# Another order of a head pair's steps: chosen rows' values and the second head's turn in their own pair, rows of maxima sent ahead of loads

## The chip, the cores and the metric

The kernel runs on one core of one Trainium2 chip. A core has five engines that each run a list of instructions of their own: TensorE (PE, matrix products and transposes; its weight loads are shown as PEld), VectorE (DVE), ScalarE (ACT), GpSimd (POOL) and SyncE (SP), which here only sends transfers to 16 DMA engines. They wait for one another by semaphores. The metric is the device time of one execution in microseconds (us), lower is better.

## What is computed

A transformer layer on 2 x 1024 tokens of 512 numbers: LayerNorm, attention with 16 heads of 32, LayerNorm and residual, then a mixture of 8 experts with a shared part, LayerNorm and residual. The edit touches the attention only:

```python
ctx = _local_attention(q, k, v)      # each block of 128 queries sees 256 keys around it
idx = _global_index(q)               # 62 rows with the largest norm of q, the first and the last row
qg = jnp.take_along_axis(q, idx[..., None], axis=-2)
g_scores = jnp.einsum('nhqd,nhkd->nhqk', qg, k) / math.sqrt(d)     # 64 chosen rows see all 1024 keys
g_probs = jax.nn.softmax(g_scores, axis=-1)
g_ctx = jnp.einsum('nhqk,nhkd->nhqd', g_probs, v)
ctx = ctx.at[bn, bh, idx].set(g_ctx)
x = x + _layernorm(ctx_as_tokens, axis=-1)
```

## The kernel before

Three stages follow one another. The projections of q, k and v (to about 169 us) write them to HBM, split in high and low parts. The attention (169 to 384 us) takes the 2 x 16 heads in 16 pairs. The experts take the rest. While the attention runs, the slots of each pair hold chores of the other stages: the search for the largest norms of the second batch (pairs 0 to 5, on VectorE), loads of expert weights, and from pair 10 on the LayerNorm of finished tokens.

A head has these steps. Its queries and keys are loaded by SyncE, three DMAs each (load_queries, load_keys); values come for two pairs at a time (load_values). TensorE makes the scores once for the maximum of each row (row_max, two units into a 1024 wide buffer), VectorE takes the maxima (row_reduce), TensorE turns them (row_shift), ScalarE copies them out (row_copy) and SyncE sends them as row 96 of the query tile (row_send). With this row in place TensorE makes the transposed, shifted scores (local_scores, four units), ScalarE the exponentials (local_exp), TensorE the products with the values (local_values), ScalarE copies them (local_out), TensorE turns them back (local_turn), VectorE divides (local_finish). After every fourth head SyncE stores the results (store_heads).

The chosen rows are done for the two heads of a pair together: gather and stack_split on GpSimd, stack_q on TensorE, stack_copy on ScalarE, global_scores, global_max, global_exp, three global_turn with three global_turned, global_values, global_out, global_back, global_finish, and scatter_rows into the stored result.

Which step stands where is written by hand, for each engine one list per pair: pair_on_pe, pair_on_act, pair_on_dve, pair_on_pool and pair_on_sp. The calls head(name, n, s, ...) and pair(name, n, ...) put the step of head 2n + s, or of pair n, at that place; slot(k) holds the chores. An engine works through its list in order, so a step that must wait holds up all that stands behind it, and a DMA is sent only when SyncE comes to it. Buffers are rings: ST_ (three banks, taken by local_scores, row_shift, stack_q, global_turn, global_back and LayerNorm turns, in TensorE's order), W_ (two wide buffers, taken by row_max, global_scores, global_values), O_ (one bank: local_values and local_turn), six query and six key tiles (QSe, KSe, QSl, KSl, and four that lie in the tiles WQH and WKH). Whoever takes a buffer waits until its last user is done. Most matrix products have one line, L1216, so they are told apart by their tiles: bank<-QS,KS are local_scores, wide<-KS,QS row_max, bank<-PT,VS local_values, wide<-KS,GT global_scores, wide<-PTG,VS global_values, bank<-twice global_back. L1311 is row_shift, L1317 stack_q, L1350 local_turn, L1374 global_turn, L1225 the turn of a LayerNorm tile.

Of the kernel before, what the change touches and what calls it, by code (L numbers as in the profile page):

```python
# [117 lines left out]
def sandwich(nc, x, wq, bq, wk, bk, wv, bv, wg, w1, w3, w2, s1, s3, s2, out):  # L118
# [16 lines left out]
    with ExitStack() as top:  # L135
# [253 lines left out]
        def places():  # L389
# [361 lines left out]
            def last_tile():  # L751
                hold["st", 15] = STC.take()
                for c in range(2):
                    hold["last", c] = UP.take()

            walk(locals())


# [7 lines left out]
        def walk(steps, engine=None):  # L766

            def do(name, *a):
                if name in steps:
                    steps[name](*a)  # L770
# [94 lines left out]
            def head(name, n, s, *a):  # L865
                h = 2 * n + s
                if (4 if name[:4] == "load" else 2 if name[:3] == "row" else 0) <= h < 32:
                    do(name, h, *a)

            def pair(name, n, *a):  # L870
                if name == "load_values":
                    if n % 2 == 0 and 2 <= n < 16:
                        do(name, n // 2)
                elif name == "scatter_rows":
                    if n % 2 == 1 and 0 <= n < 16:
                        do(name, n // 2)
                elif {"gather": 8, "stack_split": 2}.get(name, 0) <= n < 16:
                    do(name, n, *a)

            def pair_on_pe(i, slot):  # L880
                pair("global_values", i - 1)
                slot(0)
                slot(1)
                head("local_scores", i, 0, 1)
                head("local_turn", i - 1, 1)
                pair("global_scores", i)
                pair("global_back", i - 1)
                head("local_scores", i, 0, 2)
                head("row_max", i + 1, 0, 1)
                slot(2)  # L890
                head("local_scores", i, 0, 3)
                head("local_scores", i, 1, 0)
                slot(3)
                head("local_values", i, 0, 0)
                head("local_values", i, 0, 1)
                head("local_values", i, 0, 2)
                head("local_values", i, 0, 3)
                head("row_shift", i + 1, 0)
                head("row_max", i + 1, 1, 0)
                pair("global_turn", i, 0)  # L900
                slot(4)
                head("local_scores", i, 1, 1)
                head("local_turn", i, 0)
                head("local_scores", i, 1, 2)
                head("row_max", i + 1, 1, 1)
                head("local_scores", i, 1, 3)
                pair("global_turn", i, 1)
                slot(5)
                pair("stack_q", i + 1)
                head("local_values", i, 1, 0)  # L910
                head("local_values", i, 1, 1)
                head("local_values", i, 1, 2)
                head("local_values", i, 1, 3)
                head("row_max", i + 2, 0, 0)
                head("local_scores", i + 1, 0, 0)
                pair("global_turn", i, 2)
                head("row_shift", i + 1, 1)
                slot(6)
                slot(7)

            def pair_on_act(i, slot):
                slot(0)
                pair("global_out", i - 1)
                slot(1)
                head("local_exp", i, 0, 1)
                head("local_exp", i, 0, 2)
                slot(2)
                slot(3)
                head("local_exp", i, 0, 3)
                pair("global_exp", i)  # L930
                head("local_exp", i, 1, 0)
                head("row_copy", i + 1, 0)
                head("local_out", i, 0)
                pair("global_turned", i, 0)
                head("local_exp", i, 1, 1)
                slot(4)
                head("local_exp", i, 1, 2)
                slot(5)
                head("local_exp", i, 1, 3)
                pair("global_turned", i, 1)  # L940
                pair("stack_copy", i + 1)
                head("local_exp", i + 1, 0, 0)
                head("row_copy", i + 1, 1)
                pair("global_turned", i, 2)
                slot(6)
                head("local_out", i, 1)
                slot(7)

            def pair_on_dve(i, slot):
                slot(0)  # L950
# [14 lines left out]
                head("row_reduce", i + 2, 0, 0)  # L965

            def pair_on_pool(i, slot):
                pair("gather", i + 2)
                slot(0)
                slot(1)  # L970
                pair("stack_split", i + 1)
                pair("scatter_rows", i - 2)
                slot(2)
                slot(3)
                slot(4)
                slot(5)
                slot(6)
                slot(7)

            def pair_on_sp(i, slot):  # L980
                slot(0)
                slot(1)
                slot(2)
                head("store_heads", i - 1, 1)
                head("load_keys", i + 3, 0)
                head("row_send", i + 1, 0)
                pair("load_values", i + 2)
                slot(3)
                slot(4)
                slot(5)  # L990
                slot(6)
                head("load_queries", i + 2, 1)
                head("load_keys", i + 2, 1)
                head("row_send", i + 1, 1)
                head("store_heads", i, 0)
                head("load_queries", i + 3, 0)
                slot(7)

            pair_on = {"PE": pair_on_pe, "ACT": pair_on_act, "DVE": pair_on_dve, "POOL": pair_on_pool, "SP": pair_on_sp}

            def pairs(engine, with_chores=True):
# [210 lines left out]
        def tensor_program(pe):  # L1212
# [277 lines left out]
            def attention_over():  # L1490
                PE["ended"] = PE["end"]

            walk(locals(), "PE")

        def scalar_program(sc):
# [181 lines left out]
            def attention_over():  # L1679
                ACTE["ended"] = ACTE["end"]  # L1680

            walk(locals(), "ACT")


# [794 lines left out]
```

## Time and profile before

| | us |
|---|---|
| time, median of 3 | 806.63 |
| lowest, highest | 806.3, 814.18 |
| profiled execution | 810.11 |
| its span | 808.4 |
| TensorE busy | 773.3 |
| VectorE busy | 562.5 |
| ScalarE busy | 420.8 |
| GpSimd busy | 145.4 |

Busy times are sums over an engine's instructions; matmuls overlap their weight loads and their ends are modelled, so a share near 100% doesn't mean that TensorE is at its peak. A timeline row gives the start, the length from the start of the first to the end of the last of its instructions, the engine, the line, the operation with its tiles, and in brackets the idle time before it and what ended it. The granted clock of TensorE is 1.00 in all of the attention stage up to 380 us.

### The profile page before, as it was taken

To read this page: it belongs to the slowest core of one execution; us is meant where nothing else is said; L and a number is where in the kernel's file an instruction comes from. 1 tells how busy PE (TensorE), PEld (TensorE's weight loads), DVE (VectorE), ACT (ScalarE), POOL (GpSimd) and SP (SyncE) were. 2 spreads that over 40 slices of the span, in tenths; PEclk is the share of its full clock that TensorE was granted. 3 is DMA by queue.
4 is the path that set the end of the run, shared out by engine and by line. 5 is a ranking of instruction groups with operands and counts; after the bars stand their busy time and mean duration, and the time that the engine had idled before them with its cause. 6 is when DMAs were issued, how large, how long until landed. Compare 5 with 4: busy or idle time off the path is not lost. (4 is left out here: it accounts for less than half of the span.)

```text
span 808.4 us, 13818 instructions
## 1 busy us (share of the span) xinstructions
PE 773.3 (96%) x5077; PEld 650.2 (80%) x5077; DVE 562.5 (70%) x1200; ACT 420.8 (52%) x840; POOL 145.4 (18%) x229
## 2 busy tenths in 40 slices
PE   6999999999999999999999998999999999999994
PEld 4787787777777777787878886999999999887884
DVE  5764898578897567777588445566676666758676
ACT  5464352445656566677354343666676666633120
POOL 3300010510101213233254422000000000013122
PEclk9999999999999999999999999999999999999998
DMA  7789565976766798862259432586778786546444
GB/s 233 227 273 349 187 181 177 271 221 175 217 183 183 179 255 244 236 179 82 94 194 337 185 132 70 179 261 211 211 206 265 207 263 208 170 152 200 139 157 144
DMA packets 117636, 162.39 MB, mean 201 GB/s; under 512 B 17380, under 2 KB 65508, under 8 KB 117568
## 3 DMA queue, kind: packets, MB, share of 16 engines
q1 hardware_dynamic: 113984, 153.54, 62.7%
q0 software_dynamic: 3584, 7.97, 3.3%
q8 instruction: 40, 0.66, 0.3%
q14 instruction: 28, 0.23, 0.1%
HBM read 107.24 MB, written 55.05 MB: 201 GB/s over the span
## 5 line engine op out<-in xcount | busy, mean ns | idle before, releaser
L1576 ACT ACTIVATE PT<-bank 128x512 f32<-128x512 f32 x128 | 74.2, 596 | 54.7 <-PE bank L1216 50.5
L1216 PE MATMUL wide<-W2H,HH 128*128 128x512 f32 x308 | 100.7, 392 | 0.5 <-ACT OUTR L1501 0.5
L1984 DVE TENSOR_TENSOR SIL<-bank,SIL 128x256 f32<-128x256 f32 (+1 forms) x72 | 36.8, 512 | 70.9 <-ACT SIL L1661 70.5
L1661 ACT ACTIVATE SIL<-bank 128x256 f32<-128x256 f32 (+1 forms) x72 | 32.6, 453 | 100.4 <-PE bank L1216 95.3
L1216 PE MATMUL bank<-XT,W13H 128*128 128x256 f32 (+1 forms) x336 | 76.6, 322 | 0.0
L1501 ACT ACTIVATE HH<-SIL 128x256 fp32r<-128x256 f32 (+1 forms) x72 | 35.2, 489 | 64.8 <-DVE SIL L1984 64.8
L1216 PEld LDWEIGHTS wide<-W2H,HH 128*128 128x128 f32 x308 | 57.8, 188 | 13.0 <-ACT OUTR L1501 1.3
L1216 PE MATMUL wide<-W2L,HH 128*128 128x512 f32 x168 | 65.8, 391 | 0.4 <-DVE W2L L1895 0.4
L1986 DVE TENSOR_TENSOR HH<-SIL,HH 128x256 fp32r<-128x256 f32 (+1 forms) x72 | 37.0, 514 | 39.9 <-ACT HH L1501 38.5
L1216 PEld LDWEIGHTS bank<-XT,W13H 128*128 128x128 f32 x336 | 55.0, 188 | 4.7
L1216 PE MATMUL bank<-WQL,W13H 128*128 128x256 f32 (+1 forms) x168 | 55.5, 330 | 0.0
L1216 PE MATMUL bank<-WKL,W13H 128*128 128x256 f32 (+1 forms) x168 | 54.3, 323 | 0.0
L1216 PE MATMUL bank<-WQL,W13L 128*128 128x256 f32 (+1 forms) x168 | 54.1, 322 | 0.0
L1216 PE MATMUL bank<-XT,W13L 128*128 128x256 f32 (+1 forms) x168 | 53.6, 319 | 0.0
L2098 POOL TENSOR_TENSOR STC<-STC,mhalf 128x1 f32<-128x1 f32 x47 | 28.4, 604 | 134.4 <-DVE STC L1695 133.8
L2202 POOL DMA_INDIRECT H2A<-scr_oe,FG x8 | 8.0, 996 | 209.7 <-issue 209.7
L1891 DVE TENSOR_TENSOR W13L<-R,W13H 128x512 fp32r<-128x512 f32 x70 | 44.1, 685 | 1.7 <-ACT W13H L1501 1.7
L1216 PE MATMUL bank<-XT,WQH 128*128 128x256 f32 (+1 forms) x192 | 43.0, 319 | 0.0
L1216 PE MATMUL bank<-WVH,HT 128*128 128x512 f32 x128 | 41.7, 415 | 0.7 <-DVE HT L1717 0.6
L1895 DVE TENSOR_TENSOR W2L<-R,W2H 128x512 fp32r<-128x512 f32 x60 | 41.1, 686 | 1.5
L1216 PE MATMUL bank<-HT,WKH 128*128 128x512 f32 x128 | 41.0, 402 | 0.0
L1216 PE MATMUL bank<-HT,WQH 128*128 128x512 f32 x128 | 40.8, 400 | 0.0
(303 smaller groups left out, 2066.2 us busy)
## 6 DMA issues: line engine op xcount, KB each, us to landing
R<-in_L_ffn_W_dram SPq DMA_DIRECT2D x48, 512.0 KB, 5.3
scr_q<-hl SPq DMA_DIRECT2D x16, 512.0 KB, 3.7
scr_k<-hl SPq DMA_DIRECT2D x16, 512.0 KB, 4.0
R<-in_L_ffn_sw_dram SPq DMA_DIRECT2D x12, 512.0 KB, 5.0
QSe<-scr_q SPq DMA_DIRECT2D x36, 128.0 KB
KSe<-scr_k SPq DMA_DIRECT2D x36, 128.0 KB
R<-_attn_hidden_states_dram SPq DMA_DIRECT2D x16, 256.0 KB, 3.7
scr_qtok<-H2A SPq DMA_DIRECT2D x16, 256.0 KB, 3.7
```

Of the source, the lines that this page charges most:

```text
L1216: return pe.matmul(ps, a, b, start=start, stop=stop, skip_group_check=True)
L1501: return sc.activation(dst, src, ACT.Copy)
L1576: sc.activation(pt.buf[:, :], hold["s", n, u].buf[:, :], ACT.Exp, scale=SCALE).then_inc(*a_exp.up(n, u))
L1661: sc.activation(sil.buf[r, 0:N], a_in, ACT.Silu).then_inc(*a_inner.up("silu", q, m))
L1891: dv.tensor_tensor(lo, rb[:, :, c * P:(c + 1) * P], f(hi), ALU.subtract).then_inc(*d_split.up("13", j, c))
L1895: dv.tensor_tensor(W2L[:, m, :], r2[:, m, :], f(W2H[:, m, :]), ALU.subtract).then_inc(*d_split.up("2", j, m))
L1984: dv.tensor_tensor(sil[r, 0:N], b_in, sil[r, 0:N], ALU.mult).then_inc(*d_inner.up("mul", q, m))
L1986: dv.tensor_tensor(lo, sil[r, 0:N], f(HH[r, 0, m, 0:N]), ALU.subtract).then_inc(*d_inner.up("lo", q, m))
L2098: po.tensor_tensor(st[:, 2:3], st[:, 3:4], mhalf[:, :], ALU.pow).then_inc(*g_pow.up(*key))
L2202: po.indirect_dma_start(out=ga.buf, out_offset=None, in_=oed, in_offset=bass.IndirectOffsetOnAxis(ap=FG[:, t:t + 1], axis=0)).then_inc(*l_ ...
```

## The change

The lists of four engines get another order; VectorE's list is as before. No step is added or removed.

```diff
             def pair_on_pe(i, slot):
-                pair("global_values", i - 1)
+                head("local_scores", i, 0, 1)
+                pair("global_back", i - 1)
                 slot(0)
+                pair("global_scores", i)
                 slot(1)
-                head("local_scores", i, 0, 1)
-                head("local_turn", i - 1, 1)
-                pair("global_scores", i)
-                pair("global_back", i - 1)
                 head("local_scores", i, 0, 2)
                 head("row_max", i + 1, 0, 1)
...
                 pair("global_turn", i, 0)
-                slot(4)
                 head("local_scores", i, 1, 1)
                 head("local_turn", i, 0)
                 head("local_scores", i, 1, 2)
+                slot(4)
                 head("row_max", i + 1, 1, 1)
+                pair("global_turn", i, 1)
                 head("local_scores", i, 1, 3)
-                pair("global_turn", i, 1)
+                head("row_max", i + 2, 0, 0)
+                pair("stack_q", i + 1)
                 slot(5)
-                pair("stack_q", i + 1)
                 head("local_values", i, 1, 0)
                 head("local_values", i, 1, 1)
                 head("local_values", i, 1, 2)
                 head("local_values", i, 1, 3)
-                head("row_max", i + 2, 0, 0)
+                head("row_shift", i + 1, 1)
+                pair("global_turn", i, 2)
+                slot(6)
                 head("local_scores", i + 1, 0, 0)
-                pair("global_turn", i, 2)
-                head("row_shift", i + 1, 1)
-                slot(6)
+                pair("global_values", i)
                 slot(7)
+                head("local_turn", i, 1)
 
             def pair_on_act(i, slot):
...
                 head("local_exp", i, 1, 0)
+                head("local_out", i, 0)
                 head("row_copy", i + 1, 0)
-                head("local_out", i, 0)
                 pair("global_turned", i, 0)
                 head("local_exp", i, 1, 1)
+                head("local_exp", i, 1, 2)
                 slot(4)
-                head("local_exp", i, 1, 2)
                 slot(5)
                 head("local_exp", i, 1, 3)
                 pair("global_turned", i, 1)
                 pair("stack_copy", i + 1)
+                head("local_out", i, 1)
+                head("row_copy", i + 1, 1)
+                slot(6)
+                pair("global_turned", i, 2)
+                slot(7)
                 head("local_exp", i + 1, 0, 0)
-                head("row_copy", i + 1, 1)
-                pair("global_turned", i, 2)
-                slot(6)
-                head("local_out", i, 1)
-                slot(7)
...
             def pair_on_pool(i, slot):
-                pair("gather", i + 2)
                 slot(0)
                 slot(1)
+                pair("scatter_rows", i - 2)
+                pair("gather", i + 1)
+                slot(2)
+                slot(3)
                 pair("stack_split", i + 1)
-                pair("scatter_rows", i - 2)
...
             def pair_on_sp(i, slot):
                 slot(0)
                 slot(1)
+                head("load_keys", i + 2, 1)
                 slot(2)
-                head("store_heads", i - 1, 1)
-                head("load_keys", i + 3, 0)
+                pair("load_values", i + 2)
                 head("row_send", i + 1, 0)
-                pair("load_values", i + 2)
                 slot(3)
                 slot(4)
                 slot(5)
                 slot(6)
-                head("load_queries", i + 2, 1)
-                head("load_keys", i + 2, 1)
+                head("load_keys", i + 3, 0)
+                head("store_heads", i, 0)
                 head("row_send", i + 1, 1)
-                head("store_heads", i, 0)
+                head("load_queries", i + 2, 1)
+                head("store_heads", i, 1)
                 head("load_queries", i + 3, 0)
                 slot(7)
```

On TensorE, the end of pair 1 and the start of pair 2, from stack_q on, stood before as:

```order
L1317 MATMUL bank<-ident,GS 96x128
L1216 MATMUL bank<-PT,VSe 33x256 x6
L1216 MATMUL bank<-PT,VSe 33x128 x4
L1216 MATMUL wide<-KSl,QSe 128x192
L1216 MATMUL wide<-KSl,QSe 128x256 x3
L1216 MATMUL bank<-QSl,KSl 128x256 x2
L1374 MATMUL bank<-ident,PG 128x128
L1311 MATMUL bank<-ident,MX 72x128
L1216 MATMUL wide<-PTG,VSe 64x128 x9
L1216 MATMUL bank<-QSl,KSl 128x256 x2
L1350 MATMUL bank<-ident,OS 128x97 x4
L1216 MATMUL wide<-KSl,GT 128x512
```

and stand now as:

```order
L1216 MATMUL wide<-KSe,QSe 128x192
L1216 MATMUL wide<-KSe,QSe 128x256 x3
L1317 MATMUL bank<-ident,GS 96x128
L1216 MATMUL bank<-PT,VSe 33x256 x6
L1216 MATMUL bank<-PT,VSe 33x128 x4
L1311 MATMUL bank<-ident,MX 72x128
L1374 MATMUL bank<-ident,PG 128x128
L1216 MATMUL bank<-QSl,KSl 128x256 x2
L1216 MATMUL wide<-PTG,VSe 64x128 x9
L1350 MATMUL bank<-ident,OS 128x97 x4
L1216 MATMUL bank<-QSl,KSl 128x256 x2
L1216 MATMUL bank<-twice,OS 128x64
```

The row_max of the next pair but one went ahead of the products with the values, row_shift stands right behind them, and the turn-back of the chosen rows ahead of the next pair's scores of chosen rows.

On SyncE, after the first loads into late buffers (pair 0), a row of maxima is DMA ...<-MR. Before:

```order
L2283 DMA QSl0<-scr_q 32x1024 x3
L2292 DMA KSl1<-scr_k 32x1024 x3
L2309 DMA WQH<-MR2 1x8x128
L2301 DMA VSl<-scr_v 64x136
L2302 DMA VSl<-scr_v 128x7x136
L2304 DMA VSl<-scr_v 64x136
L2283 DMA QSl1<-scr_q 32x1024 x3
L2292 DMA KSe0<-scr_k 32x1024 x3
L2309 DMA WQH<-MR3 1x8x128
```

and now:

```order
L2283 DMA QSl0<-scr_q 32x1024 x3
L2292 DMA KSl1<-scr_k 32x1024 x3
L2301 DMA VSl<-scr_v 64x136
L2302 DMA VSl<-scr_v 128x7x136
L2304 DMA VSl<-scr_v 64x136
L2309 DMA WQH<-MR2 1x8x128
L2292 DMA KSe0<-scr_k 32x1024 x3
L2309 DMA WQH<-MR3 1x8x128
L2283 DMA QSl1<-scr_q 32x1024 x3
L2283 DMA QSe0<-scr_q 32x1024 x3
```

The row of head 2 went behind the values, the row of head 3 ahead of three loads of queries.

Around the first store of four heads (scr_ctx<-CT0), from a row of maxima on, SyncE sent before:

```order
L2309 DMA QSl1<-MR1 1x8x128
L2283 DMA WQH<-scr_q 32x1024 x3
L2351 DMA R13<-in_L0_ffn_sw1_dram 128x4x256
L2319 DMA scr_ctx<-CT0 128x8x128
L2292 DMA WKH<-scr_k 32x1024 x3
```

and now:

```order
L2309 DMA QSl1<-MR1 1x8x128
L2283 DMA QSe1<-scr_q 32x1024 x3
L2319 DMA scr_ctx<-CT0 128x8x128
L2283 DMA WQH<-scr_q 32x1024 x3
L2351 DMA R13<-in_L0_ffn_sw1_dram 128x4x256
L2292 DMA WKH<-scr_k 32x1024 x3
```

The queries of the tile WQH, which stood right behind the row, now stand behind three other loads and the store.

## Rows read from the trace of the kernel before

**Rows 1.** The page, part 1: busy us, share of the span, number of instructions.
```profile
PE 773.3 (96%) x5077; PEld 650.2 (80%) x5077; DVE 562.5 (70%) x1200; ACT 420.8 (52%) x840; POOL 145.4 (18%) x229
```

**Rows 2.** Windows: length; busy PE, PEld, DVE, ACT, POOL; clock; DMA share; GB/s.
```profile
206.20:247.06 40.86, 40.08 (x356) 31.26 (x355) 37.18 (x72) 25.72 (x58) 4.68 (x8) 1.00 0.74 201
287.98:313.88 25.90, 25.78 (x239) 20.48 (x237) 16.61 (x39) 17.03 (x39) 4.00 (x6) 1.00 0.88 244
```

**Rows 3.** Timeline of TensorE in pairs 2 and 3.
```profile
206.20 0.27 PE L1317 MATMUL bank<-ident,GS 128*96 128x128 f32 x1
...
211.61 0.50 PE L1216 MATMUL wide<-KSl,GT 96*128 96x512 f32 x1
...
216.50 0.30 PE L1311 MATMUL bank<-ident,MX 128*72 128x128 f32 x1
216.70 0.70 PE L1216 MATMUL wide<-KSl,WQH 96*128 96x192 f32 x4
```

**Rows 4.** Timeline of VectorE in the same pair.
```profile
211.48 1.20 DVE L1768 MAX8 TV<-NRM 16x8 f32<-16x1024 f32 x1
...
213.91 1.22 DVE L1842 TENSOR_REDUCE SG<-wide 128x1 f32<-128x1024 f32 x1
...
216.10 0.35 DVE L1822 TENSOR_REDUCE MX<-wide 128x1 f32<-128x192 f32 x1
217.44 0.36 DVE L1817 TENSOR_REDUCE MX<-wide 128x1 f32<-128x192 f32 x1 [1.00 <-PE wide L1216]
```

**Rows 5.** Timeline of TensorE from stack_q in pair 10 to stack_q in pair 14.
```profile
313.88 0.27 PE L1317 MATMUL bank<-ident,GS 128*96 128x128 f32 x1
...
320.83 0.60 PE L1225 MATMUL bank<-ident,H2A 128*128 128x128 f32 x4
321.18 0.58 PE L1216 MATMUL bank<-QSl,WKH 97*128 97x128 f32 x3
322.15 0.50 PE L1216 MATMUL bank<-QSl,KSe 97*128 97x256 f32 x2 [0.38 <-DMA QSl<-MR]
...
365.18 0.27 PE L1311 MATMUL bank<-ident,MX 128*72 128x128 f32 x1 [0.34 <-DVE WKL L1885]
...
368.37 0.27 PE L1317 MATMUL bank<-ident,GS 128*96 128x128 f32 x1
```

**Rows 6.** Timeline of SyncE's sending in pair 10.
```profile
315.18 0.37 SPq L2335 DMA_DIRECT2D scr_x<-XX  x1
...
317.01 1.40 SPq L2292 DMA_DIRECT2D WKH<-scr_k  x3
318.45 0.68 SPq L2309 DMA_DIRECT2D QSl<-MR  x1
```

**Rows 7.** Timeline of SyncE's sending in pair 0.
```profile
175.05 1.35 SPq L2283 DMA_DIRECT2D QSl<-scr_q  x3
...
177.83 0.65 SPq L2309 DMA_DIRECT2D WQH<-MR  x1
178.53 0.51 SPq L2301 DMA_DIRECT2D VSl<-scr_v  x1
...
179.70 0.58 SPq L2304 DMA_DIRECT2D VSl<-scr_v  x1
...
183.26 0.68 SPq L2309 DMA_DIRECT2D WQH<-MR  x1
```

**Rows 8.** Timeline of TensorE: first scores of head 2, and of head 3.
```profile
180.75 0.51 PE L1216 MATMUL bank<-WQH,WKH 97*128 97x256 f32 x2 [0.78 <-DMA WQH<-MR]
...
187.14 0.50 PE L1216 MATMUL bank<-WQH,WKH 97*128 97x256 f32 x2 [1.44 <-DMA WQH<-MR]
```

**Rows 9.** Keys behind the store; DMA issues, 180 to 385: KB each, us to landing.
```profile
200.19 2.46 SPq L2292 DMA_DIRECT2D WKH<-scr_k  x3
...
WKH<-scr_k SPq DMA_DIRECT2D x24, 128.0 KB, 4.8
...
VSl<-scr_v SPq DMA_DIRECT2D x3, 476.0 KB
```

More of the change, by code:

```diff
@@ L967, in pair_on_pool @@
             def pair_on_pool(i, slot):
-                pair("gather", i + 2)
                 slot(0)
                 slot(1)
-                pair("stack_split", i + 1)
                 pair("scatter_rows", i - 2)
+                pair("gather", i + 1)
                 slot(2)
                 slot(3)
+                pair("stack_split", i + 1)
                 slot(4)
@@ L991, in pair_on_sp @@
                 slot(6)
+                head("load_keys", i + 3, 0)
+                head("store_heads", i, 0)
+                head("row_send", i + 1, 1)
                 head("load_queries", i + 2, 1)
-                head("load_keys", i + 2, 1)
-                head("row_send", i + 1, 1)
-                head("store_heads", i, 0)
+                head("store_heads", i, 1)
                 head("load_queries", i + 3, 0)
```

## The prediction

> **What bounds the kernel now.** I read the page's busy times first: TensorE is busy for 96% of the span [rows 1]. That does not yet say that it sets the pace everywhere, since a matmul's end is modelled; the edit touches only the attention stage (about 169 to 384 us), so I cut that stage into windows and looked at which engine waits for which.
>
> The first windows differ in kind [rows 2]. From 206.20 to 247.06, three head pairs take 40.86 us, 13.62 each, and VectorE is busy for 37.18 of it (91%): this is where it also looks for the largest norms of the second batch. From 287.98 to 313.88 two pairs take 25.90, 12.95 each, TensorE is busy for 25.78 and VectorE for 16.61. So there are two regimes: VectorE sets the pace up to about 247 us, TensorE after that.
>
> What closes the circle in the first regime is seen by laying TensorE's timeline beside VectorE's. VectorE's row_reduce(i+1,0,1) ends at 216.45; row_shift follows on TensorE at 216.50, row_max(i+1,1,0) behind it at 216.70; VectorE sits idle for 1.00 us and takes that product at 217.44 [rows 3, 4]. Everything else in VectorE's pair stands back to back. A pair is thus VectorE's work plus this 1.00, and TensorE has 13.62 - 12.95 = 0.67 us of slack in it, which it spends in small waits, such as that for the reduction of the buffer (VectorE goes on at 211.48, chosen scores start at 211.61).
>
> After 313.88 the clean pair of 12.95 gets four transposes of a LayerNorm tile, 0.35 us (320.83 to 321.18), so 13.30. The four pairs from 313.88 to 368.37 take 54.49, 13.62 each [rows 5]: 0.32 too much in each, 1.3 in all. Two of them wait for a row of maxima (0.38 at 322.15, the next one is alike), two for VectorE (0.34 at 365.18).
>
> **The change, part by part.**
>
> *Values of the chosen rows and the second head's turn, in their own pair; chosen rows' turn-back ahead of the scores (TensorE, ScalarE).* No matmul is added or removed. In the VectorE regime nothing moves: VectorE's own list is the same in both kernels, and the three instructions on which it waits each pair (row_reduce, row_shift, row_max in a row) keep their neighbours. global_back a microsecond earlier frees VectorE's global_finish, but VectorE reaches it late anyway: it starts its reduction of the chosen scores at 213.91, long after the scores began at 211.61. Term: 0.0. It would only be other than 0 if a wait of more than 0.67 us per pair came in on TensorE.
>
> In the TensorE regime global_back ahead of the scores lets VectorE begin about half a microsecond sooner on the maximum, the row_reduce behind it and the LayerNorm step at the end; the 0.34 waits for VectorE go, and they are no longer than that half microsecond. Bounds: 0 and all the excess of these pairs.
>
> *Rows of maxima ahead of loads (SyncE).* In pair 10 SyncE waits for the LayerNorm store until 315.18, then sends three loads of queries and three of keys, and only at 318.45 the row; TensorE needs it and gets it at 322.15, 3.7 us later [rows 6]. In the new order only three loads stand between that store and the row, so it goes 1.4 us sooner, more than the wait of 0.38. Both DMA waits go. With the part above: -1.3 us, the whole excess, the other end being 0. I take the whole, since each wait is shorter than what is gained on its own releaser.
>
> *The other side of that: what is now ahead of a row.* row_send(i+1,0) is sent behind the values in every second pair. In the steady stage it doesn't matter: the row is sent a third into the pair and used at its end. At the start it does. All loads into late buffers wait for one fence and then come in a burst; the row of head 2 is sent at 177.83 and its first scores start at 180.75, after a wait; the row of head 3 is sent at 183.26 and used at 187.14 after a wait of 1.44 [rows 7, 8]. In the new order the three loads of values (178.53 to 180.28, 1.8 us of sending) come ahead of the row of head 2: it is sent at about 179.6. Rows took 2.9 and 3.9 us from sending to use; behind the values (476 KB and two of 34, 544 in all [rows 9]) I take the longer: 183.5. Then TensorE has to do what lies between local_scores(1,0,0) and local_scores(1,1,0): 180.75 to 185.7 (187.14 less the wait of 1.44) is 4.95, less 0.3 for two transposes that now stand before it: 188.1 against 187.14. The row of head 3 is sent earlier than now (row_shift right behind the values' products) and has landed by then. Term: +1.0 us; bounds 0.0 (row lands after 2.9) and +2.0 (a microsecond later still). Also row_max(2,0,0) now stands before the second head's values and waits for queries that are sent from 175.05 on; that wait ends near 179 and lies inside the one for the row.
>
> The Trainium skill speaks against this edit: "DMA: Bandwidth & Descriptors", section "Queues, rings and completion order", says that on each DMA engine descriptors are consumed in ring order, so a small row can't pass the 544 KB ahead of it. By the rule the term is the +1.0 or more; without it the row would land after its 2.9 us and the term would be 0. The trace agrees as far as it goes: behind six loads a row of 4 KB took 3.9 us.
>
> *Queries later.* Queries of head (i+3,0) are now sent behind the store of four heads (512 KB) in odd pairs, and row_max(i+2,0,0), which needs them, stands 1.86 us of products sooner. In the old order keys stand behind that store: sent from 200.19 to 202.65, and loads of that form take 4.8 us to land [rows 9], so near 206.7. TensorE would be at that row_max at 206.20, the place of stack_q now. A wait of 0.5 us in three pairs of the VectorE regime is inside the slack of 0.67: 0.0. In the TensorE regime the store is sent earlier in the pair, since VectorE, whose division comes before it, isn't behind: 0.0. Upper bound: 1.0 us in each of six pairs.
>
> *GpSimd.* The gather moves from a pair ahead to just before its split and behind the scatter. The row of indices is there two microseconds or more before stack_q; 0.0, at most 0.3 in two odd pairs.
>
> **Sum.** 0.0 + 1.0 - 1.3 + 0.0 = -0.3 us on the attention stage. Later stages start from its end and move with it. The profiled execution took 810.11 us outside, 808.4 of span, 3.5 above the median of 806.63; the difference goes onto the median: 806.3.
>
> **Rivals.**
>
> A. *As forecast*, small terms of both signs: 805 to 808. Chance 0.62.
>
> B. *The queries are late.* TensorE waits at row_max(i+2,0,0) in pairs 2, 4, 6 and 8, 10, 12. With 1.0 us each: 3 x (1.0 - 0.67) + 3 x 1.0 = +4.0, 810.3: slower than before. It decides from 0.67 us of wait in the first three, from the first tenth in the others. For it: DMA engines are busy for 0.74 to 0.88 of these windows [rows 2]. Against: the hand count gives 0.5 and 0. Chance 0.17, of which 0.07 for waits near 2 us, 3 x 1.33 + 3 x 2 = +10, 816.
>
> C. *The VectorE regime is shortened too.* If VectorE's wait of 1.00 went, six pairs would come down by 0.67: -4.0, with the -1.3 and no loss at the start 801.3. Against: the neighbours row_shift and row_max are unchanged. Chance 0.13, with 0.03 for yet more.
>
> D. *ScalarE is late.* The copy of the chosen rows' product (global_out) must lie between global_values and global_back, and only the turn and one unit of scores are left there, 0.6 us, where the scores of the chosen rows stood too. If this costs 0.15 in ten pairs: +1.5, 807.8. Chance 0.08.
>
> **How the numbers follow.** About 1% (8 us) is what a measurement of this kernel can tell from no change. All the waits named here together are 4.0 of slack in six pairs, 1.3 late and 0.78 + 1.44 at the start, 7.5 us, so faster by over 1% gets 0.03, a part of C. Slower by over 1% needs the heavy end of B: 0.07. The rest, 0.90, is within 1%. The range of 801 to 811.5 takes in A, D, C and B's middle; outside it are the heavy end of B and the tail of C.
>
> **What would show it.** Right: pairs of 13.6 us up to 247, VectorE's 1.00 before L1817 still there; no wait for MR rows after 313 and pairs of 13.3 there; a longer wait for WQH<-MR near 183. Wrong: TensorE idle before row_max on the wide buffers until a load of QS (B); VectorE's idle time before L1817 gone (C); L1216 bank<-twice waiting for ScalarE's OS (D).

## The result, and the profile after

| | ratio to before, 95% interval | median us (lowest to highest) | profiled execution, its span | TensorE busy |
|---|---|---|---|---|
| before | 1 | 808.08 (806.3 to 814.18) | 810.11, 808.4 | 773.3 |
| changed | 1.0311 [1.0238, 1.0385] | 834.74 (830.31 to 837.67) | 834.02, 832.3 | 783.3 |

The changed kernel is 3.1% slower, some 26 us, where 806.3 with a range up to 811.5 had been forecast. The page of after, part 1 and the clock of part 2 (busy us and share of the span as in [rows 1]; below it the granted clock in 40 slices of 20.8 us, in tenths, 9 for 90% and more):

```profile
PE 783.3 (94%) x5077; PEld 658.7 (79%) x5077; DVE 562.6 (68%) x1200; ACT 421.9 (51%) x840; POOL 145.7 (18%) x229
...
PEclk9999999999799987999999999999999999999998
```

Against [rows 1] VectorE, ScalarE and GpSimd did the same work to within a microsecond, but TensorE was busy for 10 us longer with the same 5077 products. So the loss has two parts, waiting and slower work. Behind the attention nothing was lost: its last part was 424 us before and is 421 now. All that is sought lies in the attention stage, which ends 27 us later.

TensorE's waits in that stage (engine, line, what was waited for; us in all, times, longest):

```profile
PE bank L1216 <- DMA QSe<-MR: 8.4, 2, 5.0
PE bank L1216 <- DMA QSl<-MR: 6.6, 2, 4.0
PE bank L1216 <- DMA WQH<-MR: 3.8, 2, 2.9
PE wide L1216 <- DMA QSl<-scr_q: 1.8, 1, 1.8
```

Six waits for a row of maxima, 18.8 us, and one of 1.8 for queries at the start; all the others are small. They stand at one step, local_scores(i+1, 0, 0), and only in the stretches in which SyncE also sends values. Windows of after from stack_q to the next stack_q; the second is the first such stretch with a wait (columns as in [rows 2]):

```profile
193.68:207.32 13.64, 13.17 (x120) 10.37 (x119) 12.42 (x24) 8.57 (x20) 2.16 (x3) 1.00 0.56 153
207.32:228.21 20.89, 17.47 (x120) 13.43 (x119) 12.44 (x25) 8.71 (x20) 0.81 (x4) 0.75 0.70 162
228.21:241.83 13.62, 13.17 (x121) 10.37 (x119) 12.40 (x25) 8.57 (x20) 2.23 (x4) 1.00 0.54 152
241.83:257.22 15.39, 12.79 (x120) 10.18 (x119) 12.52 (x24) 8.63 (x20) 0.72 (x3) 1.00 0.89 210
...
300.75:324.20 23.45, 18.48 (x121) 14.22 (x119) 7.69 (x17) 8.47 (x20) 1.08 (x3) 0.71 0.61 155
```

The stretches between them are as forecast (13.64, 13.62) or better. The ones with values, in us:

| stretch from stack_q of pair | 2 | 4 | 6 | 8 | 10 | 12 | sum |
|---|---|---|---|---|---|---|---|
| before | 13.58 | 13.65 | 14.46 | 13.02 | 13.70 | 13.53 | 81.94 |
| after | 20.89 | 15.39 | 17.20 | 23.45 | 18.81 | 14.38 | 110.12 |
| wait for the row in it | 3.42 | 2.60 | 2.87 | 4.97 | 4.04 | 0.91 | 18.81 |
| granted clock in it | 0.75 | 1.00 | 0.90 | 0.71 | 0.91 | 1.00 | |

They are 28.2 us longer in all; the other stretches together give 1.9 back and the start takes 0.7, which makes the 27. In pairs 4 and 12, where the clock stays at 1.00, a stretch grows by no more than its wait. In pairs 2 and 8, where it falls for long, it grows by twice as much. (The 14.46 of before in pair 6 hold a wait of 1.03 us for VectorE that the same list of TensorE doesn't show in experiment 10, 13.02, so that this pair's loss is put too low by about that.) TensorE's timeline of after around that of pair 2:

```profile
209.38 0.30 PE L1311 MATMUL bank<-ident,MX 128*72 128x128 f32 x1
209.52 0.27 PE L1374 MATMUL bank<-ident,PG 128*128 128x128 f32 x1
213.21 0.50 PE L1216 MATMUL bank<-QSe,KSe 97*128 97x256 f32 x2 [3.42 <-DMA QSe<-MR]
...
219.48 1.32 PE L1216 MATMUL bank<-QSe,KSe 97*128 97x128 f32 x5
220.73 3.63 PE L1216 MATMUL bank<-PT,VSl 128*33 128x256 f32 x20
...
225.58 0.48 PE L1216 MATMUL bank<-QSe,KSe 97*128 97x256 f32 x2
```

The products with the values take 3.63 us here and 1.93 at the full clock: the lower of the two clock levels (granted clock 0.50 in windows of 2 us from 216 to 224, 0.69 and 0.75 in those beside them), for some 10 us behind a wait of 3.42. In pairs 6 and 10 the means of 0.90 and 0.91 come to some 3.4 us at the lower level.

And SyncE's sending of after before that wait:

```profile
200.36 0.38 SPq L2319 DMA_DIRECT2D scr_ctx<-CT  x1
200.79 2.20 SPq L2283 DMA_DIRECT2D WQH<-scr_q  x3
203.03 0.43 SPq L2351 DMA_DIRECT2D R<-in_L_ffn_sw_dram  x1
203.56 1.37 SPq L2292 DMA_DIRECT2D WKH<-scr_k  x3
205.03 0.51 SPq L2301 DMA_DIRECT2D VSe<-scr_v  x1
205.58 0.58 SPq L2302 DMA_DIRECT2D VSe<-scr_v  x1
206.21 0.62 SPq L2304 DMA_DIRECT2D VSe<-scr_v  x1
206.87 0.68 SPq L2309 DMA_DIRECT2D QSe<-MR  x1
```

The row goes at 206.87 and is there at 213.2, 6.3 us later. The same place in the kernel before, and the first scores that need the row:

```profile
197.06 1.37 SPq L2283 DMA_DIRECT2D WQH<-scr_q  x3
198.47 0.43 SPq L2351 DMA_DIRECT2D R<-in_L_ffn_sw_dram  x1
199.71 0.38 SPq L2319 DMA_DIRECT2D scr_ctx<-CT  x1
...
203.64 0.64 SPq L2309 DMA_DIRECT2D QSe<-MR  x1
...
208.83 0.40 PE L1216 MATMUL bank<-QSe,KSl 97*128 97x256 f32 x2
```

Queries and weights went ahead of the store, three loads of keys behind it (200.19 [rows 9]), and then nothing: SyncE waited for the row itself, sent it at 203.64, and sent the values behind it. What that pause did is seen in the busy share of the DMA engines (tenths). Before from 203 to 209 us, then after from 206 to 213 us, 40 slices each; in both the row is sent in the fifth slice:

```profile
DMA  9999999795644110005304558999999999998599
```

```profile
DMA  9999999999597979979999999999999999899989
```

Before, the engines ran dry 1.3 us behind the row's sending. After, they stay full until well past its landing.

### The profile page after: what moved, and what is told of

It reads as the page before. It is cut to its first block and busy times, and to the rows that moved or that the text cites. A ratio compares the mean times of both kernels' runs of the same rounds, so it can differ in the third digit from the quotient of the medians.

```text
span 832.3 us, 13846 instructions
## 1 busy us (share of the span) xinstructions
PE 783.3 (94%) x5077; PEld 658.7 (79%) x5077; DVE 562.6 (68%) x1200; ACT 421.9 (51%) x840; POOL 145.7 (18%) x229
```

## The experiments

In the comparison above and the three below, the kernel before took 808 to 815 us (chips differ), so the ratios count, not the microseconds.

**1. The row ahead of the values, nothing else.**

```diff
-                pair("load_values", i + 2)
                 head("row_send", i + 1, 0)
+                pair("load_values", i + 2)
```

> The changed kernel with one swap on SyncE: row_send(i+1, 0) goes ahead of load_values(i+2) instead of behind it. Theory Q (a queue): the lost time comes from that row alone, which in every second pair is sent 1.85 us later and then lies behind 544 KB of values. Then in pair 2 it goes at about 205.0 and lands some 3 us later, before TensorE needs it at 209.8; the waits of 3.42, 2.60, 2.87, 4.97, 4.04 and 0.91 us for a row of maxima in the pairs 2 to 12 go, the granted clock stays at 1.00, and the time is 804 to 808. Rival S (the store and what stands behind it): the row is late because SyncE waits for the store of four heads at 200.36 and then sends seven loads ahead of it; only the 1.85 us of sending come off, waits of 1 to 3 us remain and the time is 815 to 825. Rival T (the order on TensorE): the time stays above 830.

Measured 810.06, ratio 0.9984 [0.9955, 1.0013]: one swap takes away all of the loss. Four waits of this row remain: 0.84 us in pair 2 (the stretch takes 13.62 all the same), 1.22, 1.59 and 0.52 later; behind the one of 1.59, in pair 10, the granted clock fell to 0.90 for the stretch, which takes 16.39. Theory Q holds for the size; S is right only in that a small rest stays.

**2. The reverse: the kernel before, with the values ahead of the row.**

> The kernel before with one swap on SyncE: load_values(i+2) ahead of row_send(i+1, 0). This is the step of which the prediction said that it doesn't matter in the steady stage. As the prediction has it: 806 to 808. Theory Q: the row of pair 2, ready at 203.6, goes at about 205.5 instead of 203.64 and needs 5 us and more behind the values, so it is there at about 211; the kernel before wants it at 208.83. That is 2 us of wait in each of six pairs, less 0.67 of slack in three of them: +8 to +12, 815 to 820, and above that if the granted clock falls behind the waits. Rival S: the values alone do little, below 811.

Measured 820.45, ratio 1.0087 [1.0057, 1.0117]. The direction is theory Q's and the step of the prediction is wrong, but theory Q said too much for the early pairs: in pair 2 the wait is 0.59 us and the stretch 13.76, in pair 4 there is no wait for it. Of the profiled execution's loss 5.6 us lie at the start (a wait of 3.34 for the row of head 2, and the clock falls behind it) and 2.8, 3.3 and 1.2 in pairs 6, 8 and 10. So the values alone don't make 3%. They do it on top of something that the changed list adds and this one doesn't.

**3 and 4. The SyncE lists exchanged.**

> The changed kernel with the whole SyncE list of before, the lists of TensorE, ScalarE and GpSimd as changed. Theory Q or S (SyncE's list holds the whole loss): 803 to 808, the late pairs a little shorter than before (12.7 to 13.3 us). Rival T (TensorE's new order holds a part of it): above 812.

Measured 808.39, ratio 0.9953 [0.9909, 0.9997], span 804.5 against 808.4.

> The kernel before with only the SyncE list changed. Theory Q or S: 820 to 840, waits for a row of maxima in every second pair. Rival T: below 815.

Measured 844.17, ratio 1.0417 [1.0378, 1.0457], with seven waits for rows, 20.3 us. Rival T falls: the whole loss is in SyncE's list, and the new order of TensorE, ScalarE and GpSimd is by itself a small gain, if any (the interval ends at 0.9997). With the old order of TensorE the new SyncE list is even worse: its stretches with values are as long as in the changed kernel (109.8 us), but the row of head 2 is waited for at the start (3.73 us; the start takes 3.1 more) and the stretches without values take 1.8 more.

**6 and 7. Bytes or sending time?** The three loads of values are split around the row.

```diff
                 pair("load_values", i + 2)
                 head("row_send", i + 1, 0)
+                pair("values_rest", i + 2)
```

> The changed kernel, but of the three loads of values only the two small ones (34 KB each) are sent ahead of row_send(i+1, 0); the one of 476 KB goes behind it. If it is the 544 KB ahead of the row that count: near the kernel with the row ahead of all values, 808 to 813. If it is the time that SyncE needs to send three loads (1.85 us, of which two thirds remain): 818 to 826.

> The changed kernel, but of the three loads of values only the one of 476 KB is sent ahead of row_send(i+1, 0), the two small ones behind it. If it is the bytes that count: near the changed kernel, 826 to 835. If it is the time that SyncE needs for sending (a third of it remains): 812 to 818.

With 68 KB ahead of the row: ratio 0.9997 [0.9964, 1.003]. With 476 KB ahead: 1.0266 [1.0216, 1.0316]. Two sends of 34 KB keep SyncE busy for longer than one of 476 KB (1.1 us against 0.4), and the time shows no cost of them. It is the bytes. (The profiled execution with 68 KB does have waits: five for this row, of 0.4 to 2.2 us, and in pair 9 one of 2.44 us for queries before row_max, which is the prediction's rival B; it did not occur in the changed kernel.)

**9. The values in another queue.**

```diff
             def pair_on_act(i, slot):
...
                 head("local_exp", i, 0, 3)
+                pair("values_act", i + 2)
                 pair("global_exp", i)
```

> The changed kernel, but from pair 2 on ScalarE sends the three loads of values, behind local_exp(i, 0, 3), about 1.5 us before SyncE comes to row_send(i+1, 0). The row still has the 544 KB of values started ahead of it on the same 16 DMA engines, but in another queue. If what holds the row is the order within SyncE's queue: it lands some 3 us after it is sent, as in the kernel before, and the time is 804 to 814, ScalarE's sending included. If it is the DMA engines themselves, which the values keep busy whoever sends them: waits of 2 us and more for rows of maxima stay in the even pairs, 820 to 835.

Measured 821.77, ratio 1.0143 [1.0099, 1.0187], between the two theories in size, and much of it lies elsewhere. ScalarE's global_exp now comes some 2 us late, and TensorE waits 0.8 to 1.0 us for it in six stretches without values. In the profiled execution the stretches without values lose 5.2 us, those with values 5.7, and the start 7.7 (a wait of 2.62 for the row of head 2, and the clock at 0.68 behind it), though SyncE sends the values there as in the changed kernel. The landing tells more. SyncE and TensorE in pair 2 of this kernel:

```profile
212.93 0.64 SPq L2336 DMA_DIRECT2D QSe<-MR  x1
...
219.72 0.50 PE L1222 MATMUL bank<-QSe,KSe 97*128 97x256 f32 x2 [0.84 <-DMA QSe<-MR]
```

The row takes 6.8 us with no values ahead of it in its own queue, and 6.6 in pair 8. In pair 2 SyncE's own queue holds ahead of it what it holds in experiment 1. From the store's sending to the first scores it is 10.3 us there (199.11 to 209.38), 12.3 here (207.46 to 219.72) and 12.9 in the changed kernel. So the values in ScalarE's queue delay the row by 2 us, nearly what they cost in its own; order within SyncE's queue is not enough to explain that.

**A sum for all of them.** After these runs I counted what is ahead of the row from the store on (SyncE waits for VectorE before it): store 512 KB, keys 384; in the changed list also queries 384, expert weights 512 and values 544. At the 243 GB/s that a window of before shows,

```profile
202.00:210.00 8.00, 7.85 (x81) 6.26 (x79) 6.93 (x13) 5.65 (x14) 2.52 (x4) 1.00 0.86 243
```

and 2.9 us for the row itself [rows 7, 8], the first scores can start at (1 KB is 1024 bytes):

| kernel, pair 2 | store sent | KB ahead | sum gives | first scores |
|---|---|---|---|---|
| 1, row ahead | 199.11 | 1792 | 209.6 | 209.38 |
| 6, 68 KB ahead | 199.16 | 1860 | 209.9 | 209.44 |
| 7, 476 KB ahead | 200.80 | 2268 | 213.3 | 212.31 |
| changed | 200.36 | 2336 | 213.1 | 213.21 |
| 4, new SyncE list | 203.58 | 2336 | 216.3 | 215.47 |
| 9, values on ScalarE | 207.46 | 2336 | 220.2 | 219.72 |
| 2, before with values ahead | 205.48 | 1440 | 214.5 | 215.37 |

All seven are within a microsecond; the sum was made after the runs, so this is a fit and no forecast. Number 9 comes out only if the values of the other queue are counted: without them the sum gives 217.9 in pair 2 and 247.2, 275.7 and 303.2 in pairs 4, 6 and 8, with them 249.5, 278.0 and 305.5, and the scores started at 248.97, 277.31 and 305.24.

The start of the count matters in the lists of before. There the queries and weights (896 KB) are sent just ahead of the store, 197.06 to 198.9, and are not done when the store goes. Counted from 197.06, 1792 KB end at 204.6, which is where the slices above fall, so the row, sent at 203.64, can be there at 207.5, 1.3 us before 208.83 where it is needed. Experiment 2 counted so gives 215.6 in pair 2 (215.37 measured) and 270.3 in pair 6 (270.05), where the count from the store would give 268.4. Two places stay off: in pair 8 of the changed kernel the sum gives 305.9 and the row came at 308.2, and in pair 8 of experiment 2 it is 301.1 against 302.6, so there something is left over that isn't found.

This also explains why 2 cost so little and 1 gained so much. The 1.3 us to spare in before take more than half of the 2.3 us that the values need (544 KB at that rate). In the changed list the queries and weights had already used them up: sent behind the store, they leave the DMA engines less to do before it (share 0.39 in 197 to 199 us of before) and more between it and the row, and even without the values the row comes late by 0.84 us (experiment 1).

**5. Is the clock a cost of its own?** 26 transposes of a constant in each of five waits.

```diff
+                if r == 2 and i in (2, 4, 6, 8, 10):
+                    for k in range(26):
+                        c = (1 + k % 3) * P
+                        pe.transpose(tb.buf[:, c:c + P], ident[:, :], ident[:, :])
                 for k, t in enumerate(TILES[r]):
```

> The changed kernel, with 26 transposes of a constant that nobody reads ahead of global_turn(i, 2) in the pairs 2, 4, 6, 8 and 10, where TensorE waits for the row of maxima anyway; at the 0.35 us of four such transposes they are 2.3 us of work in each. Theory K (the clock adds to the waits): the waits of the changed kernel are 18.8 us in all, but the even pairs are 29.1 us longer than before; the rest is TensorE at half speed behind the wait (values in 3.63 instead of 1.93 us). With TensorE busy in the wait the granted clock stays at 1.00 in more of these pairs, pair 2 comes from 20.89 down to about 17, pair 8 from 23.45 to about 18.5, and the whole takes 822 to 828 although work was added. Rival (the waits alone, the work behind them is slow for another reason, such as late copies or a busy memory): 833 to 840.

Measured 828.4, ratio 1.0158 [1.0111, 1.0204]: useless work was added, and half of the loss went. Its profiled execution took 835.87 us, more than its median, so I read stretches and not its end. TensorE in pair 2, and two windows, pairs 2 and 8:

```profile
209.94 3.00 PE L1375 MATMUL bank<-ident 128*128 128x128 f32 x26
212.78 0.27 PE L1378 MATMUL bank<-ident,PG 128*128 128x128 f32 x1
213.34 0.50 PE L1216 MATMUL bank<-QSe,KSe 97*128 97x256 f32 x2 [0.29 <-DMA QSe<-MR]
...
218.19 1.93 PE L1216 MATMUL bank<-PT,VSl 128*33 128x256 f32 x20
```

```profile
207.74:223.65 15.91, 15.62 (x147) 13.03 (x145) 12.45 (x25) 9.02 (x20) 0.84 (x4) 1.00 0.81 202
...
296.44:312.59 16.15, 15.61 (x146) 12.92 (x146) 8.00 (x18) 8.75 (x19) 1.35 (x3) 1.00 0.89 224
```

The row is as late as in the changed kernel (213.34, and 213.21 there). But TensorE was busy meanwhile, the clock stayed at 1.00, and the stretch takes 15.91 instead of 20.89. So of the 7.3 us that this stretch had lost, 5.0 were the clock and 2.3 the wait. Theory K holds for pairs 2 and 8. (Its expectation has the stretches 29.1 us longer than before; by the table it is 28.2.) The cure is no better than the wait in every place. In pair 4, where the clock had not fallen, the row came later still behind the filler (a wait of 1.55) and the stretch takes 17.19 for 15.39; in pair 10 of the same execution a wait of 2.94 us stood behind the filler, and the clock fell to 0.78 for that stretch, 23.54 us; pair 12, without filler, takes 17.99. The six stretches with values together are only 3 us shorter here than in the changed kernel (107.0 for 110.1), so what the clock costs is shown for two pairs and not for the whole. The Trainium skill, "TensorE: Matmul & The Clock Gate", section "HAM oscillation — how this bites in real kernels", describes such a loop: waits for a DMA between bursts of products bring the throttled clock back each time. The trace agrees for four waits of the changed kernel (0.71 to 0.91 in their stretches) and not for those of 2.60 and 0.91 us, behind which it stayed at 1.00. The length of the wait doesn't decide it: the clock also fell behind 2.07 us (experiment 7, pair 2, 0.74 in the stretch) and 1.59 (experiment 1, pair 10), and stayed at 1.00 behind 3.10 (experiment 2, pair 8).

**8 and 12. A version that beats both.** The lists of experiment 3, and on VectorE, where it waits for row_max:

```diff
                 slot(4)
+                if i < 6:
+                    slot(5)
                 head("row_reduce", i + 1, 1, 0)
                 head("local_finish", i, 0)
-                slot(5)
+                if i >= 6:
+                    slot(5)
```

> Meant to beat both: TensorE, ScalarE and GpSimd as changed, SyncE as before (which took 808.39 against 812.88 in the same runs), and on VectorE in the pairs 0 to 5 one step of the search for the largest norms (1.2 us) stands ahead of row_reduce(i+1, 1, 0), in the 1.00 us in which VectorE waits there. By the reading of the prediction (a pair of these is VectorE's work and that wait, TensorE has 0.67 us of slack) the pairs 2 to 6 come from 13.6 down to 12.95 or so: 3 to 4 us less than e3_old_sync. Rival: the step pushes row_reduce(i+1, 1, 0) and what hangs on it (row_max two units on, the row of the second head) back by as much as it gains: no change against e3_old_sync.

> e8_chore_in_gap again, the same kernel, beside the two above and with more rounds: 0.983 to 0.990 of the kernel before. If the first result was partly the chip's doing, it comes nearer to the ratio of the two profiled spans, 800.0 to 808.4, 0.990.

Measured 802.37, ratio 0.985 [0.9805, 0.9895], and the second time 801.1, 0.9899 [0.9858, 0.994]. One stretch of the early pairs, where before had 13.6:

```profile
193.06:205.55 12.49, 12.49 (x120) 10.13 (x119) 12.27 (x24) 8.56 (x20) 0.00 (x0) 1.00 0.71 194
```

TensorE is busy for all of it, and VectorE for 12.27. The others of the early pairs take 12.48 to 12.86.

**10. The same on the kernel before.**

> The kernel before, with VectorE's step of the search for the largest norms ahead of row_reduce(i+1, 1, 0) in the pairs 0 to 5, nothing else. It prices the 1.00 us that VectorE waits in each of these pairs, with TensorE's old order: by the prediction's reading TensorE has 0.67 us of slack, so the pairs come from 13.6 to 12.95 and not below, -3 to -4 us in all, and the 12.49 of e8_chore_in_gap are due to TensorE's new order. If instead the pairs here come down to 12.5 too, TensorE's order has nothing to do with it.

Measured 805.12, ratio 0.9947 [0.9922, 0.9972]. Three early pairs, to be laid beside the first row of [rows 2]:

```profile
205.42:244.12 38.70, 38.52 (x356) 30.86 (x355) 36.85 (x72) 25.71 (x58) 4.99 (x8) 1.00 0.79 211
```

12.90 a pair, as the reading of the two regimes had it (12.95), and not 12.49. The rest of experiment 8 is the new order of TensorE, ScalarE and GpSimd; the next experiment shows a part of it at work, in the pairs that VectorE doesn't bound.

**11. The turn-back of the chosen rows ahead of the scores, alone.**

```diff
-                pair("global_scores", i)
                 pair("global_back", i - 1)
+                pair("global_scores", i)
```

> The kernel before with one swap on TensorE: global_back(i-1) ahead of global_scores(i). This is the part that the prediction credited with the end of the 0.34 us waits for VectorE in the late pairs. If it is right: no wait of row_shift for VectorE after 313, pairs 12 and 14 shorter by 0.3 us, 0.7 in all, no change in the pairs up to 247. If it is wrong: those waits stay, and the shorter pairs of e3_old_sync (12.5 to 13.1 where there were 12.9 to 13.5) come from other parts of TensorE's list.

The two waits of row_shift for VectorE, 0.7 us before, are gone behind 313, but the two stretches with them are shorter by 0.14 and 0.11 only, where 0.3 each had been expected. What was not expected: the stretches of pairs 7 to 9, which had no marked wait, take 12.6 us where they took 12.9 to 13.0. VectorE in one of these, before:

```profile
307.47 0.51 DVE L1854 TENSOR_SCALAR GC<-bank,SG 64x32 f32<-64x32 f32 x2 [0.45 <-PE bank L1216]
...
310.21 0.35 DVE L1822 TENSOR_REDUCE MX<-wide 128x1 f32<-128x192 f32 x1
```

and TensorE behind it, again before:

```profile
308.64 1.93 PE L1216 MATMUL bank<-PT,VSl 128*33 128x256 f32 x20
310.61 0.30 PE L1311 MATMUL bank<-ident,MX 128*72 128x128 f32 x1
310.81 0.70 PE L1216 MATMUL wide<-KSe,QSl 96*128 96x192 f32 x4
```

The same with the swap:

```profile
304.55 0.51 DVE L1854 TENSOR_SCALAR GC<-bank,SG 64x32 f32<-64x32 f32 x2
...
307.28 0.35 DVE L1822 TENSOR_REDUCE MX<-wide 128x1 f32<-128x192 f32 x1
```

```profile
306.12 1.93 PE L1216 MATMUL bank<-PT,VSl 128*33 128x256 f32 x20
307.97 0.30 PE L1311 MATMUL bank<-ident,MX 128*72 128x128 f32 x1
308.03 0.72 PE L1216 MATMUL wide<-KSe,QSl 96*128 96x192 f32 x4
```

Before, VectorE waits 0.45 us for global_back, ends its reduction at 310.56, and row_shift comes 1.97 us behind the start of the values' products and row_max 0.20 behind that; now VectorE is done at 307.63, and it is 1.85 and 0.06. That is 0.26 us of TensorE's time in this pair, in waits too short for the trace to mark. Timed the swap is 810.14, ratio 0.9996 [0.9966, 1.0025], so what the traces show (0.3 us in each of three pairs, 0.1 to 0.35 in three of the later ones, and 0.56 lost in pair 10) is below what the timing can tell.

## Why the prediction was wrong, step by step

**The step that failed** is one sentence: "In the steady stage it doesn't matter: the row is sent a third into the pair and used at its end." Already for the old order the reading is wrong: from the row's sending to its use it was 5.2 us (203.64 to 208.83) in a pair of 13.65, so the row went some 60% of the way in and not a third. The step also takes the moment of sending from the old order, in which SyncE pauses for the row, and it takes a landing of about 3 us for granted. In the new order the row goes 3.2 us later (206.87 against 203.64) and needs 6.3 us, where TensorE came for it 2.9 us behind its sending. The term stood at nothing; the stage paid 27 us, nearly all of it here: 18.8 of waits, and lower clock behind four of them (5.0 us in pair 2, by experiment 5).

**The rule was at hand and used in one place.** The prediction weighed the Trainium skill's "DMA: Bandwidth & Descriptors", section "Queues, rings and completion order", by which each DMA engine takes the descriptors of a ring in order, for the start, where it gave +1.0. The same 544 KB stand ahead of the same kind of row in six more pairs. Experiments 6 and 7 agree with the rule. Experiment 9 goes beyond it: 6.8 us with the values in the other queue.

**What else was ahead of the row** wasn't counted. "Queries later" was costed only for who needs the queries; nobody did have to wait for them in the steady stage, as forecast. That 384 KB of queries and 512 KB of weights had moved from ahead of the store to behind it, between SyncE's wait at the store and the row, was not in the sum. The share of 0.74 and 0.88 of busy DMA engines was cited for rival B only, and spoke for this case much more.

**The start** was right in size by luck and wrong in place. Forecast +1.0; from the first stack_q to the third, at the end of pair 1, it was 0.7 us longer (24.99 against 24.30). The row of head 2 went at 179.63, forecast 179.6, and the scores started at 182.89, forecast 183.5, with no wait at the row. The wait was at row_max, for its queries (1.75 us, until 178.98), which the prediction had put inside the other one. Behind it the granted clock fell to 0.50 (181.5 to 183.5 us), and the products with the values took 2.82 us, which the prediction didn't have either.

**Two regimes and the slack** were right. 13.64, 13.62 and 13.54 us in the three early stretches without values; a wait of 2.60 in pair 4 cost 1.7, its length less 0.9, near the 0.67 of slack; and experiment 10 came to 12.90 for 12.95.

**The -1.3** for the late pairs was right in sign where no values are sent. In the changed kernel the stretches without values from pair 7 on take 12.79, 12.69, 13.02 and 12.65 for 12.91, 12.88, 13.76 and 13.50 before. The other half of the term, that no wait for a row is left behind 313, failed: pairs 10 and 12 wait 4.04 and 0.91 us for it. The part on global_back named the right mechanism (VectorE's wait of 0.45 us goes in experiment 11), but applied it only to the 0.34 us waits. The "clean pair" of 12.95 was not clean: 0.3 us of unmarked waits went with the swap.

**Rivals.** In the changed kernel B (queries), C and D did not occur. D did in other runs with TensorE's new order: waits of 0.3 to 1.1 us of global_back for ScalarE in experiments 1, 3, 6 and 8, such as 0.73 and 0.34 in experiment 3. That slower by over 1% got 0.07, all of it from B, is the consequence of the failed step: the mechanism that decided was not among the rivals.

What stays open: the 2.3 us by which the row of pair 8 came later than the sum, the exact share of the clock in the pairs other than 2, and what decides behind which waits it falls.

## What to carry to other kernels

In this kernel a small, urgent transfer had to be priced by the bytes sent since the DMA engines were last idle, over the rate that the windows show, whoever sent them; not by its place in the list. It is worth doing this sum first. A pause of the sending engine just ahead of it can be what makes it fast, and loads that fill such a pause must go behind it. Where a wait of some microseconds falls on a TensorE that is otherwise busy, look at the granted clock behind it before setting the loss to the length of the wait; and before moving a step, ask of every wait on another engine what could stand in it.

## What the runs showed of the hardware

The clock behind a wait cost more than the wait itself in pair 2: 5.0 us behind one of 3.42, taken back by 26 transposes that nobody reads. The length of a wait doesn't tell whether the clock falls: 3.10 us (experiment 2) and 2.60 left it at 1.00, while 2.87, 2.07 (experiment 7) and 1.59 (experiment 1) were followed by 0.90, 0.74 and 0.90 in their stretches. Once fallen, it stayed down for some 3.4 us in pairs 6 and 10 and some 10 in pair 2.

Loads in ScalarE's queue delayed a row in SyncE's by about as much as loads in its own queue: in pair 2 the scores started at 219.72, by the sum 220.2 with those bytes and 217.9 without, and pairs 4, 6 and 8 are alike.

TensorE's 12.95 us for a pair, with 25.78 us busy in 25.90 [rows 2], looked like its limit and held waits that no row marks: it is 12.6 with one swap (experiment 11) and 12.5 for the same products in experiment 8, where the window again shows it busy throughout. The busy share of a window doesn't show such waits; the distances between the starts of neighbouring rows did (0.12 and 0.14 us in experiment 11).
